# Background projection by halves of a tile, inside a fused attention kernel

## The chip, the cores and the metric

The kernel runs on one core of one Trainium2 chip. The metric is the time of one execution on the device in microseconds (us), as the median of the runs. The engines are TensorE (PE in the profile, with its weight loads as PEld), VectorE (DVE), ScalarE (ACT), GpSimd (POOL) and SyncE (SP), which here only issues transfers.

## The reference, cut to what matters

Two transformer blocks on x of 4 batches x 2048 tokens x 256 features, 16 heads of 16. The change lies in the first attention alone:

```python
q, k, v = split(x @ qkv_w.T)                       # 16 heads of 16
scores = alpha * tanh(q @ k.T / beta)
bits = tanh(x @ hex_w.T); hexc = tanh(x @ q6_w.T)  # 6 + 6 features a token
scores += lam * (bits @ bits.T) / 2 + (hexc @ Mh @ hexc.T) / 6 * gate
out = softmax(causal(scores)) @ v
```

Behind it come the output projection with residual and layer norm, a feed-forward layer, a second attention (rope, plain softmax) and a second feed-forward layer.

## The kernel before, in words

The phases run one after the other: `setup_phase`, `project_phase` (q, k, v and features of batch 0 only), `attend_phase` for layer 0, `middle_phase`, `attend_phase` for layer 1, `post1_phase`. The change is in `attend_phase`, and all but one constant of it concerns layer 0.

**Passes and steps.** A pass (`it`, 16 in all) is one batch and four heads. It has 34 steps (`even_steps`, line 595), each one block of 128 keys against 512 queries for four heads. The queries of a pass are four groups of 512; group 0 ends at step 3, group 1 at 8, group 2 at 20, group 3 at 33. Steps 0, 1, 3, 7, 8, 17, 18, 20, 32 and 33 touch the causal diagonal and add a mask by further matmuls; 1, 3, 8, 18, 20 and 33 of them consist of two pieces. The global step is S = 34 * it + s, up to N = 544.

**A step on each engine, layer 0.** TensorE (from line 892): `weigh(S-2)`, probabilities times v, four heads in 16 matmuls (line 887, bank 6 or 7 by group); `extra(S, 0)` and `extra(S, 1)` (line 864, masks in line 866), the feature part of the scores for two heads; background pieces of place "a"; `scores(S+1)` of four heads (line 854); `extra(S, 2)`; background pieces of place "b"; `extra(S, 3)`. The extra products have two banks in turn: number h waits for VectorE's sum number h-2. ScalarE (line 924): tanh of the scores of S (line 929, 2048 columns), then exp of step S-1 (line 940, 2048 columns), which waits for all four sums of S-1. VectorE, in `sums` (line 993): the copy of a background tile if one ended in this step (`evict`, line 952); sums 0 and 1 (line 1004: alpha * tanh + extra product, read from PSUM); one part of a group's normalisation (`normalise`, line 964); sums 2 and 3. The four parts are a transpose out of PSUM (line 971, counter `o_tr`), a reciprocal (974), a multiplication (978) and a transpose (982, counter `o_n`). The last one waits until the stores of the group before last (`o_out`) have landed, since they read the same buffer `on_s`. Parts become due three steps behind the end of a group, one a step.

**Background projection.** Passes 0 to 11 (NX = 12) also project one group of 512 tokens of a later batch: features (g), q and k in two tiles each, the mixed features f in two tiles, and v in two. The list `plan` gives the places (step and a or b) of the matmuls of each tile. Each tile is copied once, by `evict` at the start of VectorE's step in which its last matmul stands, and the copy waits for that matmul (`bg_ps`). The next tile's first matmul waits for the copy (`bg_ev`). For q, k and f tiles GpSimd then splits the copy in three bf16 parts with four instructions (lines 1033, 1036, 1038, 1040; counters `hi`, `rest`, `mid`, `low`). The feature tile goes through a tanh of ScalarE (line 922) and not through VectorE.

**SyncE's queue** is one list in order (loop in line 781), where each item waits for its counter: at S the load for the group that ended at S-4 (14 transfers, lines 585, 725 and 726, behind `o_tr`); the store of a background tile that ended at S-5; the four stores of the group that ended at S-7 (`store_o`, line 759, transfers of line 765, behind `o_n`).

Of the kernel before, what the change touches and what calls it, by code (L numbers as in the profile page):

```python
# [24 lines left out]
B, T, D = 4, 2048, 256  # L25
# [586 lines left out]
def attend_phase(nc, kn, layer, w=None):  # L612
# [13 lines left out]
    LAG = 2  # L626
    QU, KU = 3, 6
    QK0, E0, O0 = 0, 4, 6
    tiles = [("g", 0), ("q", 0), ("q", 1), ("k", 0), ("k", 1), ("f", 0), ("f", 1)]
    NTL = len(tiles)  # L630
    kinds = tiles + [("v", 0), ("v", 1)]
    NU = len(kinds)
    NX = (B - 1) * GB if layer == 0 else 0
    plan = ["9a 9b", "12a 12b 12b 13a", "13b 14a 14b 15a", "15b 16a 16b 19a", "24a 24b 24b 25a", "25b 26a", "26b 27a", "27b 28a 28b 29a", "29b 30a 30b 31a"]
    slots = {}
    for u, places in enumerate(plan):
        places = places.split()
        for i, p in enumerate(places):
            slots.setdefault(p, []).append((u, i, i == len(places) - 1))
    bank_of = {u: O0 + (1 if 1 <= u <= 3 else 0) for u in range(NU)}  # L640
    behind = {0: 0, 1: 1, 4: 2}
    ahead = {2: 0, 3: 3, 0: 8}

    def pieces(S, place):

        it, s = divmod(S, NST)
        return [(it * NU + u, i, last) for u, i, last in slots.get(f"{s}{place}", [])] if 0 <= it < NX else []

    def unit_at(S):

        ended = [j for j, i, last in pieces(S, "a") + pieces(S, "b") if last]
        return ended[0] if ended else None

    def unit(j):

        X, u = divmod(j, NU)
        kind, m = kinds[u]
        return X, kind, m, X * NTL + u, {"q": P, "k": P, "f": 96, "g": NF, "v": P}[kind], bank_of[u]
    SR, FR = (QROWS, FROWS + 3) if layer == 0 else (QROWS + 3, 0)
    with ExitStack() as ctx:  # L660
        ph = Phase(nc, ctx, f"att{layer}")
# [52 lines left out]
        def _(sp):  # L714
# [18 lines left out]

            def store_unit(j):

                X, kind, m, tile, n, bank = unit(j)
                b, gq = X // GB + 1, X % GB
                if kind == "v":
# [35 lines left out]
            for n in range(QU):  # L774
                load(n)
                if layer == 0 and n == 0:
# [26 lines left out]
        def _(pe):  # L803
# [1 line left out]
                c.start(pe)  # L805
            pe.wait_ge(ones_in, 16)

            def project(j, i, done):

                X, kind, m, tile, n, bank = unit(j)  # L810
                if i == 0:
                    if j == 0:
                        pe.wait_ge(w_in, 64)
# [3 lines left out]
                    if j % NU in behind:  # L817

                        o_tr.wait(pe, X * GB + behind[j % NU])
                half, c = divmod(i, DC)  # L820
                cols = slice(half * D, (half + 1) * D)
                if kind == "f":
                    cols = slice(i * D, (i + 1) * D)
                    mm = pe.matmul(ps[0:n, bank, cols], kn["Cq"][:].rearrange("p q e h -> p (q e h)")[:, m * n:(m + 1) * n], f12[:, X % 2, cols], start=True, stop=True)
                elif kind == "g":
                    mm = pe.matmul(ps[0:n, bank], w12_s[:, c, :], xt_s[:, X % 2, c], start=c == 0, stop=c == DC - 1)
                elif kind == "v":
                    at_t = slice((2 * m + half) * P, (2 * m + half + 1) * P)
                    mm = pe.matmul(ps[:, bank, cols], xt_s[:, X % 2, c, at_t], wv_s[:, c, :], start=c == 0, stop=c == DC - 1)
                else:  # L830
                    lhs = (wq_s if kind == "q" else wk_s)[:, c, m * P:(m + 1) * P]
                    mm = pe.matmul(ps[0:n, bank, cols], lhs, xt_s[:, X % 2, c, cols], start=c == 0, stop=c == DC - 1)  # L832
                if done:
                    bg_ps.done(mm)

            def pieces_at(S, place):
                for j, i, last in pieces(S, place):
                    project(j, i, last)

            def scores(S, pair):  # L840
                it, _, pieces, _ = at(S)
# [50 lines left out]
            for S in range(N + LAG):  # L892
# [4 lines left out]
                if layer == 0 and S < N:  # L897
                    extra(S, 0)
                    extra(S, 1)
                    pieces_at(S, "a")  # L900
                    if S + 1 < N:
                        scores(S + 1, 0)
                if S + 1 < N:
                    scores(S + 1, 1)
                if layer == 0 and S < N:
                    extra(S, 2)
                    pieces_at(S, "b")
                    extra(S, 3)

        @block.scalar  # L910
        def _(act):
# [2 lines left out]

            def feature(j):

                X, kind, m, tile, n, bank = unit(j)
                if kind == "g":
                    bg_ps.wait(act, j)
                    if X >= 2:  # L920
# [22 lines left out]
        def _(dve):  # L943
# [7 lines left out]

            def evict(j):

                X, kind, m, tile, n, bank = unit(j)
# [65 lines left out]
        if layer == 0:  # L1020
            @block.gpsimd
            def _(pool):
                for c in (hi, rest, mid, low):
                    c.start(pool)
                for j in range(NX * NU):
                    X, kind, m, tile, n, bank = unit(j)
                    if kind == "v":
# [1006 lines left out]
```

## Time and profile before

| | us |
|---|---|
| median of 3 runs | 4102.77 (4102.47 to 4106.52) |
| profiled execution | 4100.62 |
| its span, first to last instruction | 4098.8 |
| busy: TensorE / ScalarE / VectorE / GpSimd | 3696.2 / 3502.5 / 2527.2 / 623.6 |
| layer 0 attention, first tanh to last | 133.5 to 2284.9 |
| passes 0 to 11 (with background) | 1653.66 |
| mean granted TensorE clock | 0.97 |

How to read it: busy shares of the whole span mix six phases. For the change only the stretch from 133.5 us to 1787.2 us (passes with background) and on to 2284.9 us (passes 12 to 15, without) counts. A pass is cut from the start of its first tanh to the start of the next pass's. An instruction's duration includes a tail that overlaps the next one, so the distance of two starts is less than a duration. TensorE makes each f32 matmul of the background in two records.

### The profile page before, as it was taken

To read this page: it belongs to the slowest core of one execution; us is meant where nothing else is said; L and a number is where in the kernel's file an instruction comes from. 1 tells how busy PE (TensorE), PEld (TensorE's weight loads), DVE (VectorE), ACT (ScalarE), POOL (GpSimd) and SP (SyncE) were. 2 spreads that over 40 slices of the span, in tenths; PEclk is the share of its full clock that TensorE was granted. 3 is DMA by queue.
4 is the path that set the end of the run, shared out by engine and by line. 5 is a ranking of instruction groups with operands and counts; after the bars stand their busy time and mean duration, and the time that the engine had idled before them with its cause. 6 is when DMAs were issued, how large, how long until landed. Compare 5 with 4: busy or idle time off the path is not lost. (4 is left out here: it accounts for less than half of the span.)

```text
span 4098.8 us, 62490 instructions
## 1 busy us (share of the span) xinstructions
PE 3696.2 (90%) x22198; PEld 1474.5 (36%) x22198; DVE 2527.2 (62%) x4349; ACT 3502.5 (85%) x2970; POOL 623.6 (15%) x659
## 2 busy tenths in 40 slices
PE   5699999999999999999989699969999999999798
PEld 2233333333333333333223366622222222222575
DVE  5577877787778777877788566732232323232576
ACT  2598999998999998999999566659999999999466
POOL 3112121211121112110000055510000000000232
PEclk9799999999999999999999899979999999999899
DMA  4322232222222322221121277642222222221331
GB/s 149 116 72 71 68 87 67 78 66 85 66 75 68 87 69 73 60 85 42 38 60 33 98 191 194 156 110 67 75 72 75 75 74 71 71 78 44 115 93 52
DMA packets 274745, 340.51 MB, mean 83 GB/s; under 512 B 40142, under 2 KB 207918, under 8 KB 274161
## 3 DMA queue, kind: packets, MB, share of 16 engines
q1 hardware_dynamic: 274420, 336.38, 28.1%
q8 instruction: 179, 2.93, 0.3%
q14 instruction: 146, 1.20, 0.1%
HBM read 207.97 MB, written 128.25 MB: 82 GB/s over the span
## 5 line engine op out<-in xcount | busy, mean ns | idle before, releaser
L1004 DVE SCALAR_TENSOR_TENSOR att_prob<-att_tanh,alpha,ps 128x512 f32<-128x512 f32 x2176 | 1513.9, 741 | 348.1 <-ACT att_tanh L929 189.7
L854 PE MATMUL ps<-att_q,att_k 99*128 99x512 bf16 (+5 forms) x5120 | 1138.5, 351 | 84.0 <-DMA att_v<-v_ones 61.2
L887 PE MATMUL ps<-att_prob,att_v 128*32 128x512 f32 (+3 forms) x10240 | 1173.3, 544 | 1.9 <-ACT att_prob L940 1.9
L929 ACT ACTIVATE att_tanh<-ps,rbeta 128x2048 f32<-128x2048 f32 x544 | 1083.4, 1992 | 73.6 <-PE ps L854 63.7
L940 ACT ACTIVATE att_prob<-att_prob 128x2048 f32<-128x2048 f32 x544 | 1053.2, 1936 | 91.7 <-DVE att_prob L1004 90.7
L935 ACT ACTIVATE att_prob<-ps 128x1024 f32<-128x1024 f32 x1088 | 1054.3, 1021 | 25.9 <-PE ps L854 9.8
L864 PE MATMUL ps<-att_f,att_g 75*128 75x512 bf16 (+3 forms) x2560 | 815.2, 357 | 159.4 <-DVE att_prob L1004 148.6
L854 PEld LDWEIGHTS ps<-att_q,att_k 96*128 96x128 bf16 (+1 forms) x5120 | 415.3, 98 | 897.2 <-ACT att_prob L935 427.3
L864 PEld LDWEIGHTS ps<-att_f,att_g 75*128 75x128 bf16 x2560 | 228.8, 97 | 942.9 <-DVE att_prob L1004 908.4
L991 DVE TENSOR_TENSOR att_prob<-att_prob,keep 128x512 f32<-128x512 f32 (+1 forms) x320 | 187.5, 586 | 580.6 <-ACT att_prob L935 579.5
L887 PEld LDWEIGHTS ps<-att_prob,att_v 128*32 128x32 f32 x10240 | 216.8, 108 | 367.1 <-issue 148.4
L1912 POOL TENSOR_SCALAR post_prev<-post_xt,post_om 128x512 f32<-128x512 f32 x64 | 56.8, 905 | 1233.0 <-issue 1124.6
L866 PE MATMUL ps<-mask_kq,identb 128*128 128x128 bf16 x1024 | 212.5, 221 | 0.0
L971 DVE STREAM_TRANSPOSE att_ot<-ps 128x512 f32<-128x512 f32 x128 | 91.2, 712 | 180.3 <-PE ps L887 180.3
L1683 POOL TENSOR_TENSOR mid_x1b<-mid_x,mid_bias 128x256 f32<-128x256 f32 x64 | 44.5, 729 | 626.2 <-ACT mid_x L1282 626.2
L1033 POOL CAST att_parts<-att_raw 128x512 bf16<-128x512 f32 (+1 forms) x72 | 43.8, 609 | 580.3 <-DVE att_raw L962 537.3
L1282 ACT ACTIVATE post_x<-post_rr,post_n_nb,post_n_rs 128x256 f32<-128x256 f32 x128 | 66.4, 589 | 65.6 <-DVE post_n_nb L1271 65.6
L1033 POOL CAST att_parts<-att_f 12x512 bf16<-12x512 f32 x12 | 7.2, 599 | 731.2 <-ACT att_f L922 731.2
L962 DVE COPY att_raw<-ps 128x512 f32<-128x512 f32 (+1 forms) x72 | 49.7, 690 | 98.0 <-PE ps L832 44.5
L1494 ACT ACTIVATE mid_parts<-mid_qcos 128x512 bf16<-128x512 f32 x64 | 40.1, 626 | 81.8 <-POOL mid_qcos L1657 81.6
L866 PEld LDWEIGHTS ps<-mask_kq,identb 128*128 128x128 bf16 x1024 | 101.2, 99 | 2.6 <-issue 0.7
L1040 POOL TENSOR_TENSOR att_parts<-att_rem,att_parts 128x512 bf16<-128x512 f32 (+2 forms) x84 | 97.1, 1156 | 15.1 <-POOL att_parts L1038 15.1
(162 smaller groups left out, 2975.7 us busy)
## 6 DMA issues: line engine op xcount, KB each, us to landing
att_v<-v_ones SPq DMA_DIRECT2D x128, 256.0 KB
att_k<-k_parts SPq DMA_DIRECT2D x128, 192.0 KB
att_q<-q_parts SPq DMA_DIRECT2D x128, 192.0 KB
att_k<-k_parts SPq DMA_DIRECT2D x128, 128.0 KB
att_q<-q_parts SPq DMA_DIRECT2D x128, 128.0 KB
o_t<-att_on SPq DMA_DIRECT2D x512, 32.0 KB, 1.8
v_ones<-mid_vs SPq DMA_DIRECT2D x64, 256.0 KB, 3.3
v_ones<-att_vs SPq DMA_DIRECT2D x96, 128.0 KB, 2.1
```

The source lines that it names most:

```text
L854: mm = pe.matmul(ps[:, bank, col:col + w], keys, q_s[:, n % QU, h, q0:q0 + w], start=True, stop=True)
L864: mm = pe.matmul(ps[:, E0 + h % 2, col:col + w], g_s[:, c % KU, (kb % CB) * P:(kb % CB + 1) * P], f_s[:, n % QU, h, q0:q0 + w], start=True ...
L866: mm = pe.matmul(ps[:, E0 + h % 2, col:col + P], kn["identb"][:], kn["mask_kq"][:], start=False, stop=True)
L887: mm = pe.matmul(ps[VW * h:VW * (h + 1), O0 + n % 2, q0:q0 + w], v_s[:, c % KU, kb % CB, h * VW:(h + 1) * VW], prob[:, S % R, h, col:col + ...
L929: th.done(act.activation(tanh_s[:, S % 2], ps[:, QK0:QK0 + HQ], ACT.Tanh, scale=kn["rbeta"][:, 0:1]))
L935: pr.done(act.activation(prob[:, S % R, 2 * pair:2 * pair + 2], ps[:, bank:bank + 2], ACT.Exp, scale=float(HD) ** -0.5))
L940: pr.done(act.activation(prob[:, (S - 1) % R], prob[:, (S - 1) % R], ACT.Exp))
L971: o_tr.done(dve.transpose(ot_s[:, v].rearrange("p b n -> p (b n)"), ps[:, O0 + v]))
L991: kept.done(dve.tensor_tensor(block, block, kn["keep"][:].unsqueeze(1).unsqueeze(1).to_broadcast([P, 2, len(masked), P]), ALU.min))
L1004: sc.done(dve.scalar_tensor_tensor(prob[:, S % R, h], tanh_s[:, S % 2, h], kn["alpha"][:, 0:1], ps[:, E0 + h % 2], ALU.mult, ALU.add))
L1040: low.done(pool.tensor_tensor(parts[0:n, u, 2], rem[0:n], parts[0:n, u, 1], ALU.subtract))
L1282: ins = act.activation(dst(t), src(t), ACT.Identity, scale=self.rs[:, u, t:t + 1], bias=self.nb[:, u, t:t + 1])
```

## The change

Each q, k and v tile is now projected by halves: a unit of `plan` is a half tile of 256 columns with exactly two matmuls, one in a place "b" and one in the next step's "a", so there are 15 units a pass instead of 9, with 30 matmuls as before. The two f tiles and the feature tile stay whole. The order of the tiles is g, q0, k0, f0, f1, q1, k1, v0, v1. Each unit is copied by itself: at steps 13, 14, 15, 16 (halves), 19, 20 (f), 25 to 31 and 32 (halves). Before, whole tiles were copied at 13, 15, 19, 25, 26, 27, 29 and 31. Splitting in parts and storing still go by whole tiles, after the second half. A step that has a copy does no part of a normalisation; the feature tile doesn't count. In layer 0 the stores of a group stand 14 steps behind its end in SyncE's list instead of 7.

```diff
-    plan = ["9a 9b", "12a 12b 12b 13a", "13b 14a 14b 15a", "15b 16a 16b 19a", "24a 24b 24b 25a", "25b 26a", "26b 27a", "27b 28a 28b 29a", "29b 30a 30b 31a"]
+    plan = [("g", 0, None, "9a 9b"), ("q", 0, 0, "12b 13a"), ("q", 0, 1, "13b 14a"), ("k", 0, 0, "14b 15a"), ("k", 0, 1, "15b 16a"),
+            ("f", 0, None, "16b 19a"), ("f", 1, None, "19b 20a"), ("q", 1, 0, "24b 25a"), ("q", 1, 1, "25b 26a"), ("k", 1, 0, "26b 27a"),
+            ("k", 1, 1, "27b 28a"), ("v", 0, 0, "28b 29a"), ("v", 0, 1, "29b 30a"), ("v", 1, 0, "30b 31a"), ("v", 1, 1, "31b 32a")]
...
-    behind = {0: 0, 1: 1, 4: 2}
-    ahead = {2: 0, 3: 3, 0: 8}
+    behind = {0: 0, 1: 1, 7: 2}
+    ahead = {2: 0, 3: 6, 0: 14}
...
-            for S in range(N + 8):
+            BACK = 14 if layer == 0 else 7
+            for S in range(N + BACK):
...
-                if 7 <= S < N + 7:
-                    it, s, *_ = at(S - 7)
+                if S >= BACK:
+                    it, s, *_ = at(S - BACK)
                     for g in ends[s]:
                         store_o(it * GB + g)
...
-                    bg_ev.done(dve.tensor_copy(vs[:, m, :, :, 0:HD], ps[:, bank].rearrange("p (t h d) -> p t h d", t=2, h=H)))
+                    bg_ev.done(dve.tensor_copy(vs[:, m, half, :, 0:HD], ps[:, bank, cols].rearrange("p (h d) -> p h d", h=H)))
...
-                    bg_ev.done(dve.tensor_copy(raw[0:n, tile % 2], ps[0:n, bank]))
+                    bg_ev.done(dve.tensor_copy(raw[0:n, tile % 2, cols], ps[0:n, bank, cols]))
...
+                copied = unit_at(S)
+                if copied is not None and unit(copied)[1] == "g":
+                    copied = None
                 for h in range(HQ):
-                    if h == 0 and unit_at(S) is not None:
-                        evict(unit_at(S))
-                    if h == 2:
+                    if h == 0 and copied is not None:
+                        evict(copied)
+                    if h == 2 and copied is None:
 
                         normalise(due, 1)
```

## Rows read from the trace of the kernel before

**Rows 1.** Busy time of stretches (start:end, length; busy by engine; PEclk, DMA share, GB/s)

```profile
133.53:275.98 142.45, 125.37 (x736) 47.68 (x734) 104.53 (x154) 125.67 (x69) 24.70 (x28) 0.94 0.30 88
414.77:549.63 134.86, 123.50 (x765) 47.21 (x764) 107.50 (x161) 126.92 (x71) 24.71 (x28) 1.00 0.25 75
549.63:688.43 138.80, 127.96 (x765) 47.92 (x764) 107.71 (x161) 126.91 (x71) 24.68 (x28) 0.96 0.25 73
sum 1653.66, PE 1515.02 PEld 572.44 DVE 1287.49 ACT 1521.80 POOL 296.47; mean PE 126.25 PEld 47.70 DVE 107.29 ACT 126.82 POOL 24.71
1911.39:2035.71 124.32, 112.48 (x705) 36.26 (x705) 99.91 (x152) 124.32 (x69) 0.00 (x0) 1.00 0.17 51
383.10:393.34 10.24, 10.24 (x31) 2.75 (x31) 4.92 (x9) 5.93 (x4) 5.94 (x7) 0.50 0.29 82
```

**Rows 2.** Waits of ScalarE in pass 2: total us, times, longest

```profile
ACT att_prob L940 <- DVE att_prob L1004: 7.2, 8, 1.9
```

**Rows 3.** Timeline of pass 2, steps 30 and 31: start, us, engine, line, tiles [idle before]

```profile
535.97 0.60 PE L864 MATMUL ps<-att_f,att_g 75*128 75x512 bf16 x2
...
539.67 0.60 PE L864 MATMUL ps<-att_f,att_g 75*128 75x512 bf16 x2
540.12 0.60 PE L829 MATMUL ps<-att_wv,att_xt 128*128 128x256 f32 x2
540.80 0.69 DVE L958 COPY att_vs<-ps 128x512 f32<-128x512 f32 x1 [1.20 <-PE ps L829]
541.41 2.71 DVE L1004 SCALAR_TENSOR_TENSOR att_prob<-att_tanh,alpha,ps 128x512 f32<-128x512 f32 x4
...
542.87 0.39 PE L864 MATMUL ps<-att_f,att_g 75*128 75x512 bf16 x1 [0.27 <-DVE att_prob L1004]
543.19 1.06 PE L887 MATMUL ps<-att_prob,att_v 128*32 128x512 f32 x8
544.16 1.91 ACT L940 ACTIVATE att_prob<-att_prob 128x2048 f32<-128x2048 f32 x1 [0.58 <-DVE att_prob L1004]
544.18 0.39 PE L864 MATMUL ps<-att_f,att_g 75*128 75x512 bf16 x1
```

**Rows 4.** Timeline of pass 2, the masked steps 32 and 33

```profile
544.75 1.04 PE L854 MATMUL ps<-att_q,att_k 96*128 96x128 bf16 x8
544.77 2.81 DVE L1004 SCALAR_TENSOR_TENSOR att_prob<-att_tanh,alpha,ps 128x512 f32<-128x512 f32 x4 [0.64 <-PE ps L866]
...
548.26 2.92 DVE L1004 SCALAR_TENSOR_TENSOR att_prob<-att_tanh,alpha,ps 128x512 f32<-128x512 f32 x4 [0.68 <-PE ps L866]
```

**Rows 5.** Timelines of pass 2, steps 25 and 26, and of pass 13 (last row)

```profile
515.45 1.15 POOL L1036 TENSOR_TENSOR att_rem<-att_raw,att_parts 128x512 f32<-128x512 f32 x1 [0.28 <-POOL att_parts L1033]
515.53 1.35 DVE L978 TENSOR_TENSOR att_oq<-att_ot,att_rc 128x256 f32<-128x256 f32 x1
...
518.58 0.67 PE L824 MATMUL ps<-att_f,Cq 12*96 12x256 f32 x2
...
519.34 0.69 DVE L962 COPY att_raw<-ps 96x512 f32<-96x512 f32 x1 [1.14 <-issue]
...
1962.43 0.42 DVE L978 TENSOR_TENSOR att_oq<-att_ot,att_rc 128x256 f32<-128x256 f32 x1
```

**Rows 6.** Timeline of pass 13, step 14; last row: landing of the stores of o

```profile
1965.17 0.36 SPq L726 DMA_DIRECT2D att_v<-v_ones  x1
...
1966.09 0.70 DVE L982 STREAM_TRANSPOSE att_on<-att_oq 128x512 f32<-128x512 f32 x1
...
1966.88 1.71 SPq L765 DMA_DIRECT2D o_t<-att_on  x4
...
DMA to landing us min/median/max: 1.5/1.7/2.8
```

**Rows 7.** Timeline of ScalarE in pass 2, tanh of steps 9 and 11

```profile
447.63 2.01 ACT L929 ACTIVATE att_tanh<-ps,rbeta 128x2048 f32<-128x2048 f32 x1
...
455.71 1.95 ACT L929 ACTIVATE att_tanh<-ps,rbeta 128x2048 f32<-128x2048 f32 x1
```

More of the change, by code:

```diff
@@ L628, in attend_phase, with piece_at @@
     QK0, E0, O0 = 0, 4, 6
-    tiles = [("g", 0), ("q", 0), ("q", 1), ("k", 0), ("k", 1), ("f", 0), ("f", 1)]
+    tiles = [("g", 0), ("q", 0), ("k", 0), ("f", 0), ("f", 1), ("q", 1), ("k", 1)]
     NTL = len(tiles)
-    kinds = tiles + [("v", 0), ("v", 1)]
-    NU = len(kinds)
     NX = (B - 1) * GB if layer == 0 else 0
-    plan = ["9a 9b", "12a 12b 12b 13a", "13b 14a 14b 15a", "15b 16a 16b 19a", "24a 24b 24b 25a", "25b 26a", "26b 27a", "27b 28a 28b 29a", "29b 30a 30b 31a"]
[L635 to L640, printed above, removed]
-    behind = {0: 0, 1: 1, 4: 2}
-    ahead = {2: 0, 3: 3, 0: 8}
-    def pieces(S, place):
+    plan = [("g", 0, None, "9a 9b"), ("q", 0, 0, "12b 13a"), ("q", 0, 1, "13b 14a"), ("k", 0, 0, "14b 15a"), ("k", 0, 1, "15b 16a"),
+            ("f", 0, None, "16b 19a"), ("f", 1, None, "19b 20a"), ("q", 1, 0, "24b 25a"), ("q", 1, 1, "25b 26a"), ("k", 1, 0, "26b 27a"),
+            ("k", 1, 1, "27b 28a"), ("v", 0, 0, "28b 29a"), ("v", 0, 1, "29b 30a"), ("v", 1, 0, "30b 31a"), ("v", 1, 1, "31b 32a")]
+    NU = len(plan)
+    places = {p: (u, i) for u, (_, _, _, both) in enumerate(plan) for i, p in enumerate(both.split())}
+    behind = {0: 0, 1: 1, 7: 2}
+    ahead = {2: 0, 3: 6, 0: 14}
+    def piece_at(S, place):
         it, s = divmod(S, NST)
-        return [(it * NU + u, i, last) for u, i, last in slots.get(f"{s}{place}", [])] if 0 <= it < NX else []
+        if not 0 <= it < NX or f"{s}{place}" not in places:
+            return None
+        u, i = places[f"{s}{place}"]
+        return it * NU + u, i
     def unit_at(S):
-        ended = [j for j, i, last in pieces(S, "a") + pieces(S, "b") if last]
+        ended = [found[0] for found in (piece_at(S, "a"), piece_at(S, "b")) if found and found[1] == 1]
         return ended[0] if ended else None
@@ L656, in unit @@
         X, u = divmod(j, NU)
-        kind, m = kinds[u]
-        return X, kind, m, X * NTL + u, {"q": P, "k": P, "f": 96, "g": NF, "v": P}[kind], bank_of[u]
+        kind, m, half, _ = plan[u]
+        tile = X * NTL + tiles.index((kind, m)) if kind != "v" else None
+        return X, kind, m, half, tile, {"q": P, "k": P, "f": 96, "g": NF, "v": P}[kind], O0 + (1 if 1 <= u <= 6 else 0)
     SR, FR = (QROWS, FROWS + 3) if layer == 0 else (QROWS + 3, 0)
@@ L734, in store_unit @@
             def store_unit(j):
-                X, kind, m, tile, n, bank = unit(j)
+                X, kind, m, half, tile, n, bank = unit(j)
                 b, gq = X // GB + 1, X % GB
+                if half == 0:
+                    return
                 if kind == "v":
@@ L806, in _, with project @@
             pe.wait_ge(ones_in, 16)
-            def project(j, i, done):
-                X, kind, m, tile, n, bank = unit(j)
+            def project(j, i):
+                X, kind, m, half, tile, n, bank = unit(j)
                 if i == 0:
@@ L825, in project, with piece @@
                 elif kind == "g":
[L826 to L829, printed above, removed]
-                else:
-                    lhs = (wq_s if kind == "q" else wk_s)[:, c, m * P:(m + 1) * P]
-                    mm = pe.matmul(ps[0:n, bank, cols], lhs, xt_s[:, X % 2, c, cols], start=c == 0, stop=c == DC - 1)
-                if done:
+                    mm = pe.matmul(ps[0:n, bank], w12_s[:, i, :], xt_s[:, X % 2, i], start=i == 0, stop=i == DC - 1)
+                else:
+                    cols = slice(half * D, (half + 1) * D)
+                    if kind == "v":
+                        lhs, rhs = xt_s[:, X % 2, i, (2 * m + half) * P:(2 * m + half + 1) * P], wv_s[:, i, :]
+                    else:
+                        lhs, rhs = (wq_s if kind == "q" else wk_s)[:, i, m * P:(m + 1) * P], xt_s[:, X % 2, i, cols]
+                    mm = pe.matmul(ps[0:n, bank, cols], lhs, rhs, start=i == 0, stop=i == DC - 1)
+                if i == 1:
                     bg_ps.done(mm)
-            def pieces_at(S, place):
-                for j, i, last in pieces(S, place):
-                    project(j, i, last)
+            def piece(S, place):
+                if piece_at(S, place):
+                    project(*piece_at(S, place))
             def scores(S, pair):
@@ L915, in feature @@
             def feature(j):
-                X, kind, m, tile, n, bank = unit(j)
+                X, kind, m, half, tile, n, bank = unit(j)
                 if kind == "g":
@@ L952, in evict @@
             def evict(j):
-                X, kind, m, tile, n, bank = unit(j)
+                X, kind, m, half, tile, n, bank = unit(j)
+                cols = slice(None) if half is None else slice(half * D, (half + 1) * D)
                 if kind == "v":
@@ L1025, in _ @@
                 for j in range(NX * NU):
-                    X, kind, m, tile, n, bank = unit(j)
-                    if kind == "v":
+                    X, kind, m, half, tile, n, bank = unit(j)
+                    if kind == "v" or half == 0:
                         continue
```

6 lines of the change are left out of this document (2 added, 4 removed).

## Prediction

> **What bounds the kernel now.** I read the page first: no single engine bounds the whole, so the stage is read by itself. Next come the stretches cut at the first tanh of each pass of 34 steps [rows 1]. A pass without background work takes 124.32 us, that is 3.66 us a step, and ScalarE is busy for all of it: one tanh and one exp of 2048 columns a step. So ScalarE sets the rate there. A pass with background work takes 134.86 us, but ScalarE is busy for 126.92 only. The waits of ScalarE in that pass name what it waits for: 8 waits for VectorE's sums, 7.2 us [rows 2]. There are 8 copies in a pass, so it is the copies that the change splits.
>
> Three things make up the 1653.66 us of the twelve passes. Five passes have a granted clock of 1.00 and take 134.9 to 135.2 us; the seven others have 0.94 to 0.96 and take some 138.8 [rows 1]. In those seven the clock falls to 0.50 (1.2 GHz instead of 2.4) for 10.24 us, once a pass, behind the steps in which TensorE waited most. The fall costs 138.80 - 134.86 = 3.94 us. Pass 0 has another 142.45 - 134.86 = 7.6 us of starting up. What is left, 1653.66 - 7.6 - 12 x 134.86 = 27.7 us, is the price of the lower clock. And a clean pass has 134.86 - 124.32 = 10.5 us of background.
>
> **Why a copy costs what it does.** The timeline of step 31 of pass 2 [rows 3] shows a loop through two engines. The second sum ends, the last extra product of the step starts (542.87), the weighing of an older step starts 0.32 later (543.19) and lasts 0.99 (544.18), two extra products take 0.45 (539.67 to 540.12), then comes the background piece; the copy starts 0.68 behind the start of its piece (540.80), the first sum 0.61 later (541.41). Two sums take 1.41, and the signal to TensorE 0.05. Once around with a full copy: 1.41 + 0.05 + 0.32 + 0.99 + 0.45 + 0.68 + 0.61 = 4.51 us. ScalarE's exp waits 0.58 us (544.16) for the fourth sum. Nothing in the loop is hidden by slack elsewhere: VectorE's sum of work is well under 3.65 us a step, and its queue still waits 1.20 us for the piece.
>
> **The change, part by part.** *Half copies.* 8 full copies a pass become 12 copies of 256 columns and 2 full ones (f). VectorE works on another operation of 256 columns for 0.42 us [rows 5], against 0.69 for 512 [rows 3]; I take the difference, 0.27, off the link: 0.34. A loop with a half copy then takes 4.24 us, 0.59 more than ScalarE's 3.65. Between bounds of 0.34 and 0.61 for the link I take 0.34, since both rows fit 1.05 ns a column. *First copy of a run (steps 13 and 25).* Before it stands a step with ScalarE's slack; working through it with one piece instead of two in the step before, the fourth sum is ready 0.07 us before exp wants it: 0. *The next ones* (14, 15, 16 and 26 to 31): 9 x 0.59 - 2 x 0.07 = 5.2 us. *Step 32* is masked: extra products and masks take 0.57 (544.18 to 544.75) instead of 0.45, the four sums 2.81 instead of 2.71 [rows 3, 4]: 4.46 - 3.65 = 0.8. *The f copies* stay full and stand at steps 19 and 20. A piece of f takes 0.67 against 0.60, and its copy starts 0.76 behind it [rows 5]. At 19 the transpose of the normalisation, 0.70 [rows 6], was just before in step 18 and delays the fourth sum, the second extra product and so the piece: worked through in the same way, the loop is 0.7 over. Step 20 has two pieces of mask (first sums 3.49 apart instead of 3.36 [rows 3, 4], so extra products of 0.70) and follows a copy step: 4.51 + 0.70 - 0.45 + 0.08 + 0.09 for slower sums + 0.1 for the extra product that f's piece makes late = 5.03, so 1.4 over. *Normalisation moved* to steps 17, 18, 33 and 0 of the next pass, all masked. First sum to first sum takes 3.36 and 3.49 us there; adding 0.42 and then 0.70 - 0.42, they come to 0.3 + 0.2 + 0.25 + 0.1 = 0.9. Sum of a new pass: 5.2 + 0.8 + 2.1 + 0.9 = 9.0, and the feature tile, which stays as it was: two steps from 447.63 to 455.71 instead of 7.30 [rows 7], 0.8. So 9.8 against 10.5: 0.77 us a pass before rounding, 9.2 us in twelve.
>
> What goes away and makes room for this: the multiplication in a copy step takes 1.35 us beside GpSimd's subtraction, 0.42 alone [rows 5]. After the change no such pair meets: at step 17 GpSimd's last subtraction of the k tile ends some 0.3 us before it. What this pair cost stands in the old 10.5 and not in the new 9.8.
>
> The Trainium skill speaks against this change ("VectorE: DVE Perf Modes", on the TRN2 errata): each instruction pays a fixed latency, many small tiles pay it each time, and a copy from PSUM costs 120 cycles plus one per column. The estimate from that page is 0.39 us for a half and 0.66 for a full copy; the full one's 0.69 in the trace agrees. By it, with the whole half copy in the link, a pass would be 12 x 0.05 = 0.6 us dearer, twelve of them 7 us.
>
> *Clock.* The longest stop in the passes, 1.85 us of ScalarE behind the 1.35 us multiplication, is gone; the new loops leave TensorE waiting some 0.5 us a step, as steps 29 to 33 do now at full clock. I take all 27.7 us as saved.
>
> *Stores of o, 14 steps behind instead of 7.* SyncE's queue is in order, so its place matters. The store of group 3 now stands behind the load of group 1 of the next pass, whose 14 transfers SyncE issues until 1965.17 + 0.36 = 1965.53 in pass 13 [rows 6]. Passes with copies normalise group 1 at steps 17 and 18, later than that. Passes 12 to 15 have no copies, and there the last transpose is due at step 14, at 1966.09, and it waits for those very stores, which share its buffer. Now they were made before the load. Four stores take 1.71 us to issue and land 1.7 us (up to 2.8) behind their issue: 1965.6 + 1.3 + 1.7 = 1968.6, 2.5 us late; up to 3.6 with the load's own traffic in front. Queued behind the transpose are sums 3 and 4, and ScalarE's exp and TensorE behind them. I take 2.8 us, near the usual landing, in passes 12, 13 and 14 (15 has no such load): +8.4 us. TensorE stands idle for over 2 us in each, longer than where the clock falls now; I take two falls of 3.5 us (3.94, less the background's share): +7.
>
> *The rest*: tile order, banks and the waits on o_tr stay behind events that came steps earlier; GpSimd has the same 28 instructions a pass. Price 0; a missed one would cost up to 0.6 us a pass, one late cast.
>
> **Sum.** On the profiled execution, 4100.62 us (span 4098.8): -9.2 - 27.7 + 8.4 + 7 = -21.5, 4079. The median of the runs shown is 2.15 above it: 4081.3, **4081 us**.
>
> **The rivals.** *Copies in the slack* (0.04): counted as work, a half copy fits, and the step would be as long as TensorE's, 3.70 with two pieces (535.97 to 539.67 [rows 3]). A pass then has 14 x 0.05 + 0.8 = 1.5 us of background, 8.3 less than forecast: 4081 - 12 x 8.3, near 3980. Against it stands the loop, whose every link is in order. *No late store* (0.13): had GpSimd's or SyncE's order left the buffer free, no +8.4 and +7: 4066. *Dearer links* (0.14): 0.1 us on each of 14 links in 12 passes is 17 us: 4098. *The clock falls all the same* (0.14), which ends slower: the new run of eight steps at 4.24 us has a gap of TensorE in each, and if these bring the clock down in as many passes as now, 4081 + 27.7 = 4109, in all twelve 4128. Other terms add up to +6, so the change is slower once the clock falls in six passes or more. Against it: the single steps of 4.36 to 4.5 us now run at full clock. The Trainium skill ("TensorE: Matmul & The Clock Gate", on a second failure mode) says that short, frequent idling between groups of matmuls can make the clock oscillate; the trace agrees so far that gaps of at most 0.6 us of TensorE precede the falls here. *It does nothing that counts*: part of the last two.
>
> **How the numbers follow.** My forecast has 0.55, the rivals as given. The range takes in no late store below and dearer links above, with room for landing times and one fall more or less: 4064 to 4102. A measurement of this kernel tells about 0.2%, 8.2 us, from no change, so faster means under 4094.6: forecast, cheap copies, no late store (0.72), plus 0.06 of the others, 0.78. Slower needs falls in most passes: 0.10. The rest, 0.12, is the same.
>
> **What would show it.** In passes 0 to 11: first sums 4.2 to 4.3 us apart at steps 26 to 31, 5.0 to 5.1 from 19 to 20, pass time about 134.1, clock 1.00, no multiplication over 0.5 us. In passes 12 to 14: one gap of VectorE before line 982's transpose at step 14, of 2.5 to 3.6 us, released by the stores of o, none in pass 15. It would be wrong if the loop were shorter than 4.1, if the clock rows showed 0.96 in many of the twelve passes, or if that transpose didn't wait.

## The result and the profile after

The changed kernel takes 4095.8 us (median of 20 runs, 4092.45 to 4106.26) against 4102.62 us before (20 runs, 4099.94 to 4106.62): ratio 0.9984, with a 95% interval of 0.9977 to 0.9991. So it is faster by 7 us, as that interval shows, where 21.5 were forecast; the prediction called faster only what is under 4094.6 us, and by this bound it is no change. The profiled execution took 4096.26 us.

The page and the cut by passes, for the changed kernel. The first group is of the page (busy us, share, instructions), the rows under it are busy times of stretches as in [rows 1]: passes 0 to 11 together, passes 12 to 14, then pass 2, pass 6 and a stretch inside pass 2.

```profile
span 4094.4 us, 62634 instructions
PE 3699.9 (90%) x22198; PEld 1468.8 (36%) x22198; DVE 2497.9 (61%) x4421; ACT 3515.6 (86%) x2970; POOL 623.8 (15%) x659
...
134.65:1771.96 1637.31, 1512.80 (x9139) 564.99 (x9138) 1256.50 (x1984) 1533.69 (x828) 296.58 (x336) 0.98 0.25 74
...
1771.96:2155.47 383.51, 342.35 (x2116) 110.13 (x2114) 301.24 (x459) 374.05 (x206) 0.00 (x0) 0.98 0.18 53
...
413.35:550.72 137.37, 128.03 (x766) 47.78 (x764) 104.96 (x167) 127.97 (x71) 24.73 (x28) 0.96 0.24 74
...
954.51:1088.46 133.95, 123.73 (x766) 46.33 (x764) 104.96 (x167) 127.76 (x70) 24.71 (x28) 1.00 0.25 76
...
490.85:501.09 10.24, 10.24 (x50) 3.68 (x49) 4.70 (x7) 5.57 (x4) 5.89 (x7) 0.50 0.01 3
```

A pass without a fall of the clock is now 133.95 to 134.2 us long, where the sum said 134.1 and the kernel before had 134.86 [rows 1]. But the clock still falls, in 8 of the 12 passes instead of 7, though often for a shorter time: 1637.31 - 7.6 (start of pass 0) - 12 x 134.0 = 21.7 us against 27.7 before. Passes 12 to 14 took

```profile
1787.19:2160.06 372.87, 337.22 (x2114) 108.77 (x2114) 299.77 (x457) 372.87 (x206) 0.00 (x0) 1.00 0.18 51
```

in the kernel before (the row is of its trace), so they are now 10.6 us longer. In sum: twelve passes -16.4 us, three passes +10.6 us, and 1.4 us elsewhere (the first tanh starts 1.1 us later): -4.4, the difference of the two profiled executions.

### The profile page after: what moved, and what is told of

It is laid out like the page before. It is cut to its first block and busy times, and to the rows that moved or that the text cites. A ratio compares the mean times of both kernels' runs of the same rounds, so it can differ in the third digit from the quotient of the medians.

```text
span 4094.4 us, 62634 instructions
## 1 busy us (share of the span) xinstructions
PE 3699.9 (90%) x22198; PEld 1468.8 (36%) x22198; DVE 2497.9 (61%) x4421; ACT 3515.6 (86%) x2970; POOL 623.8 (15%) x659
## 3 DMA queue, kind: packets, MB, share of 16 engines
q1 hardware_dynamic: 274420, 336.38, 27.7%
## 5 line engine op out<-in xcount | busy, mean ns | idle before, releaser
L965 DVE COPY att_raw<-ps 128x256 f32<-128x256 f32 (+1 forms) x120 | 57.2, 477 | 156.5 <-PE ps L834 86.0
```

## The loop, as it now runs

Timeline of pass 6, steps 26 and 27, of the changed kernel (start, us, engine, line, operation, tiles; idle time before in brackets):

```profile
1058.22 2.71 DVE L1010 SCALAR_TENSOR_TENSOR att_prob<-att_tanh,alpha,ps 128x512 f32<-128x512 f32 x4
...
1060.00 1.06 PE L889 MATMUL ps<-att_prob,att_v 128*32 128x512 f32 x8
...
1060.97 1.91 ACT L942 ACTIVATE att_prob<-att_prob 128x2048 f32<-128x2048 f32 x1 [0.31 <-DVE att_prob L1010]
...
1061.44 0.60 PE L834 MATMUL ps<-att_xt,att_wk 128*128 128x256 f32 x2
...
1062.12 0.42 DVE L965 COPY att_raw<-ps 128x256 f32<-128x256 f32 x1 [1.19 <-PE ps L834]
1062.47 2.71 DVE L1010 SCALAR_TENSOR_TENSOR att_prob<-att_tanh,alpha,ps 128x512 f32<-128x512 f32 x4
```

First sum to first sum: 1062.47 - 1058.22 = 4.25 us, forecast 4.24. The half copy takes 0.42 us, and the next sum starts 0.35 us behind its start, which is what it takes in the loop. VectorE is idle for 1.19 us before a copy that takes 0.42, and ScalarE for 0.31 us in each step of this run. What ScalarE waits for in pass 6:

```profile
ACT att_prob L942 <- DVE att_prob L1010: 5.1, 13, 0.7
```

Thirteen waits of 5.1 us together, where 8 of 7.2 stood [rows 2]: shorter ones, but more of them. The multiplication of the normalisation, 1.35 us beside GpSimd before [rows 5], keeps its 0.42 us throughout (min/median/max in ns):

```profile
L981 DVE TENSOR_TENSOR att_oq<-att_ot,att_rc x128: 415/424/427, 175.2 to 3794.1; 128x256 f32<-128x256 f32 x128
```

## The stall in passes 12 to 14

Timeline of pass 13, step 14, changed kernel:

```profile
1952.95 0.35 SPq L726 DMA_DIRECT2D att_v<-v_ones  x1
...
1953.43 5.58 SPq L767 DMA_DIRECT2D o_t<-att_on  x12
...
1956.51 0.71 DVE L985 STREAM_TRANSPOSE att_on<-att_oq 128x512 f32<-128x512 f32 x1 [2.57 <-DMA o_t<-att_on]
...
1957.91 0.39 PE L866 MATMUL ps<-att_f,att_g 75*128 75x512 bf16 x1 [2.52 <-DVE att_prob L1010]
1958.55 1.91 ACT L942 ACTIVATE att_prob<-att_prob 128x2048 f32<-128x2048 f32 x1 [2.44 <-DVE att_prob L1010]
```

The waits of VectorE in passes 12 to 14 (total us, times, longest):

```profile
DVE att_on L985 <- DMA o_t<-att_on: 7.7, 3, 2.6
```

The stores begin right behind the load, the transpose waits 2.57 us for them, and TensorE and ScalarE wait behind it. It happens three times and never in pass 15, as the prediction had it.

**Experiment: stores 11 steps behind.** The smallest number that puts the stores of group 3 before the load of group 1 and still keeps SyncE from waiting long for the delayed normalisations.

```diff
-            BACK = 14 if layer == 0 else 7
+            BACK = 11 if layer == 0 else 7
```

> The changed kernel with the stores of o 11 steps behind the end of a group in the first attention instead of 14, so that the stores of group 3 stand before the load of group 1 again. Theory (the stall is the place in SyncE's list): passes 12 to 14 fall from 127.3, 128.8 and 127.4 us to 124.3 each, the wait of VectorE before the last transpose at step 14 is gone, and so are the falls of the clock there; passes 0 to 11 stay. 10.7 us faster than the changed kernel, 17 faster than the kernel before (ratio 0.996). Rival (the store lands late whatever its place, or the half-clock stretches there come from elsewhere): passes 12 to 14 stay over 126 us.

Measured: 4086.25 us, ratio 0.996 to the kernel before (0.9946 to 0.9974), 9.6 us under the changed kernel's median. Passes 12 to 14, and all twelve passes before them:

```profile
1774.11:2147.17 373.06, 337.58 (x2116) 108.93 (x2113) 300.72 (x459) 373.05 (x205) 0.00 (x0) 1.00 0.19 55
...
134.14:1774.11 1639.97, 1517.32 (x9139) 565.83 (x9138) 1256.05 (x1984) 1534.02 (x827) 296.56 (x336) 0.97 0.25 74
```

The three passes are back at 373.06 us with a clock of 1.00. The wait of VectorE before the last transpose is gone. The stall cost 10.4 us, and its cause is shown: the place of four stores in one queue. The twelve passes before are 2.7 us longer than in the changed kernel, as ten of them lose the clock here and eight there, with the same instructions in them.

## What brings the clock down

The prediction let the clock stay up once the 1.85 us stop was gone. It falls in the changed kernel as well, but elsewhere: at steps 20 and 21 instead of 27. Timeline of pass 2 from the end of step 18 into step 20, TensorE's matmuls alone:

```profile
487.98 0.67 PE L825 MATMUL ps<-att_f,Cq 12*96 12x256 f32 x2
...
490.14 0.39 PE L866 MATMUL ps<-att_f,att_g 75*128 75x512 bf16 x1 [0.51 <-DVE att_prob L1010]
490.46 0.82 PE L825 MATMUL ps<-att_f,Cq 12*96 12x256 f32 x2
...
491.75 1.94 PE L889 MATMUL ps<-att_prob,att_v 128*32 128x128 f32 x16
...
495.01 1.16 PE L825 MATMUL ps<-att_f,Cq 12*96 12x256 f32 x2
```

The largest gap of TensorE here is 0.51 us; then the weighing takes 1.94 us instead of 1.06. In both kernels the two f tiles stand where the clock falls, and their matmuls feed 12 of TensorE's 128 rows (12*96 in the row). Two theories: A, it is these few rows, in steps that wait; B, it is the length of the waits. In the kernel before, steps 14 and 26 have the same stop of ScalarE, 1.85 us each. Their rows in pass 2:

```profile
467.01:472.65 5.64, 4.22 (x22) 1.86 (x23) 5.64 (x8) 3.78 (x2) 3.54 (x4) 1.00 0.35 109
514.42:520.25 5.83, 4.65 (x20) 1.33 (x20) 4.69 (x7) 3.88 (x2) 3.53 (x4) 1.00 0.54 166
```

TensorE is idle for 1.42 us in step 14 and for 1.18 in step 26. Step 14 has q pieces of 128 rows and no fall follows it in twelve passes; step 26 has f and a fall follows it in seven. That speaks for A. Five runs tell them apart.

**Experiment: f exchanged with the halves of q1.**

```diff
-    tiles = [("g", 0), ("q", 0), ("k", 0), ("f", 0), ("f", 1), ("q", 1), ("k", 1)]
+    tiles = [("g", 0), ("q", 0), ("k", 0), ("q", 1), ("f", 0), ("f", 1), ("k", 1)]
...
-            ("f", 0, None, "16b 19a"), ("f", 1, None, "19b 20a"), ("q", 1, 0, "24b 25a"), ("q", 1, 1, "25b 26a"), ("k", 1, 0, "26b 27a"),
+            ("q", 1, 0, "16b 19a"), ("q", 1, 1, "19b 20a"), ("f", 0, None, "24b 25a"), ("f", 1, None, "25b 26a"), ("k", 1, 0, "26b 27a"),
```

> The changed kernel with the two f tiles and the halves of q1 exchanged: q1's halves are copied at steps 19 and 20, f0 and f1 at steps 25 and 26. Theory A (the clock falls behind the pieces of f, which feed 12 of TensorE's 128 rows, when two tiles of f follow each other in long steps): the falls move from steps 20 and 21 to steps 26 and 27, in about as many passes, and step 20 is some 4.7 us without a fall. Theory B (it is the long masked step 20 with its waits): falls stay at steps 20 and 21. Sum without clock: step 20 shorter by 0.35, step 26 longer by 0.35: pass times without a fall within 0.3 us of 134.0 either way. Time within 10 us of the changed kernel.

Measured: 4092.82 us, ratio 0.9979 (0.9969 to 0.9989), 3 us from the changed kernel. Steps 19 to 23 and 24 to 29 of pass 6:

```profile
1024.60:1044.13 19.53, 17.60 (x122) 6.85 (x120) 14.94 (x24) 18.61 (x11) 3.54 (x4) 1.00 0.03 8
...
1044.13:1073.40 29.27, 27.77 (x115) 8.82 (x114) 18.43 (x30) 22.85 (x14) 10.59 (x12) 0.83 0.28 84
```

The falls went with f: none at 20 and 21, five at step 26 (passes 1, 3, 6, 9 and 11). Whether the place has a part in the lower number isn't shown: two kernels with the same steps 19 to 21 have eight and ten.

**Experiment: f's matmuls over 128 rows, in the changed kernel.**

```diff
-                    mm = pe.matmul(ps[0:n, bank, cols], kn["Cq"][:].rearrange("p q e h -> p (q e h)")[:, m * n:(m + 1) * n], f12[:, X % 2, cols], start=True, stop=True)
+                    mm = pe.matmul(ps[0:n, bank, cols], wq_s[:, 0, 0:n], xt_s[:, X % 2, 0, cols], start=True, stop=True)
```

> The changed kernel with f's matmuls replaced: the same number, 96 columns of weights and 256 columns of data, but over 128 rows (wq and x) instead of 12 (Cq and the features), so the mixed features of batches 1 to 3 are left out and wrong data are copied and stored in their place; all copies, waits and stores stay. Theory A (few rows of TensorE at work bring the clock down): no fall in passes 0 to 11, twelve pass times of 134 us or a little less, 21 us faster than the changed kernel, near 4075. Theory B (TensorE's waits alone do it): falls stay at steps 20 and 21 in about 8 passes and the time stays within 5 us.

Measured: 4063.04 us, ratio 0.9906 (0.9889 to 0.9922). Pass 2, and the twelve passes:

```profile
406.22:539.36 133.14, 122.72 (x766) 46.48 (x764) 104.83 (x167) 127.72 (x70) 24.73 (x28) 1.00 0.26 76
...
134.02:1739.01 1604.99, 1474.30 (x9139) 559.15 (x9138) 1253.53 (x1984) 1531.29 (x828) 296.79 (x336) 1.00 0.26 76
```

No fall in twelve passes. It came 12 us under what I expected, 10 of them because the pieces are also shorter (a pass is 133.14 instead of 134.0). So this run alone leaves B a door: the steps were shorter. In passes 12 to 14, which have no f, the falls behind the 2.5 us stall stayed: a long enough wait does it without any f.

**Experiment: the same in the kernel before.** The same line of the diff.

> The kernel before with the same replacement of f's matmuls by ones over 128 rows (mixed features of batches 1 to 3 left out, wrong data copied and stored in their place). Theory A (long steps bring the clock down only where the few-row pieces of f stand in them): no fall of the clock, twelve passes of 134 to 135 us, some 27.7 us and the shorter pieces of f off, near 4070. Theory B (the 1.85 us stop of ScalarE was what brought it down in the kernel before): falls stay at step 27 in about 7 passes, within 10 us of the kernel before.

Measured: 4069.39 us, ratio 0.9913 (0.9896 to 0.993). Steps 24 to 29 of pass 2:

```profile
501.12:527.42 26.30, 23.14 (x119) 9.05 (x118) 20.23 (x31) 22.65 (x14) 10.58 (x12) 1.00 0.34 101
```

The same stretch of pass 3 in the kernel before, where the clock falls:

```profile
641.63:672.20 30.57, 28.62 (x119) 9.61 (x118) 20.49 (x31) 22.87 (x13) 10.57 (x12) 0.83 0.34 97
```

No fall either, and the 1.85 us stop is still there (step 26 takes 5.64 us against 5.84). B said about 7 falls.

**Experiment: f over 128 rows and longer.** With the stores 11 steps behind, each f matmul stands twice.

```diff
-                    mm = pe.matmul(ps[0:n, bank, cols], kn["Cq"][:].rearrange("p q e h -> p (q e h)")[:, m * n:(m + 1) * n], f12[:, X % 2, cols], start=True, stop=True)
+                    for _ in range(2):
+                        mm = pe.matmul(ps[0:n, bank, cols], wq_s[:, 0, 0:n], xt_s[:, X % 2, 0, cols], start=True, stop=True)
```

> The changed kernel with the stores 11 steps behind and each matmul of f replaced by two over 128 rows (mixed features of batches 1 to 3 left out, wrong data stored in their place), so that a piece of f holds TensorE longer than in the changed kernel, some 0.87 us, and steps 19 and 20 are as long as with the true f or longer (5.2 us or more at 20). Theory A (few rows at work): no fall of the clock in passes 0 to 11 although the steps are no shorter. Theory B (falls went away before only because the pieces and steps were shorter): falls at steps 20 and 21 in several passes.

Measured: 4074.05 us, ratio 0.9928 (0.9906 to 0.9951). Steps 19 and 20 of pass 5, and the twelve passes:

```profile
887.39:897.14 9.75, 8.97 (x64) 4.62 (x64) 6.11 (x10) 7.71 (x5) 3.52 (x4) 1.00 0.19 55
...
132.86:1759.90 1627.04, 1495.91 (x9235) 574.98 (x9234) 1256.15 (x1984) 1533.02 (x828) 296.40 (x336) 0.99 0.25 75
```

Steps 19 and 20 are longer than in the changed kernel (9.75 us against 9.12 with the true f, in the row of the next experiment; step 20 alone 5.63 against 5.17, with a gap of TensorE of 0.62 us against 0.51), and there is no fall in any pass. (The mean of 0.99 is of the end of a low stretch at the very start of pass 0, which all kernels have.) That closes B's door in so far as longer steps and longer gaps are not enough, though these pieces also keep TensorE busy longer.

**Experiment: the pieces of q1 and k1 over 12 rows.** The other direction, with the true f and the stores 11 steps behind; the same number of matmuls, with the same columns, but 12 rows.

```diff
+                    if kind != "v" and m == 1:
+                        lhs, rhs = lhs[0:NF], rhs[0:NF]
                     mm = pe.matmul(ps[0:n, bank, cols], lhs, rhs, start=i == 0, stop=i == DC - 1)
```

> The changed kernel with the stores 11 steps behind and, in addition to f, the pieces of q1 and k1 (steps 24 to 28) cut to 12 of their 128 rows (queries and keys of half the heads' rows of batches 1 to 3 are projected from 12 features only and wrong). Theory A (few-row pieces in steps that wait): falls of the clock appear at steps 25 to 29 too, in some passes, beside those at 20 and 21; passes of 136 us and more. Theory B (few rows don't matter, the length of the waits does): the steps 25 to 28 keep 4.24 us, falls stay at steps 20 and 21 alone.

Measured (two runs): 4177.24 us, ratio 1.0183 (1.0125 to 1.0242). Steps 19 and 20 and steps 24 to 29 of pass 5, and the pass itself:

```profile
928.92:938.04 9.12, 8.46 (x58) 3.46 (x58) 6.21 (x10) 7.71 (x6) 3.52 (x4) 1.00 0.19 58
...
951.03:986.45 35.42, 34.92 (x115) 9.67 (x114) 18.26 (x30) 22.89 (x13) 7.07 (x8) 0.66 0.23 69
...
856.55:1003.49 146.94, 138.16 (x766) 47.93 (x764) 105.76 (x167) 128.18 (x70) 24.70 (x28) 0.91 0.24 69
```

Steps 24 to 29 of pass 6 in the changed kernel:

```profile
1047.66:1071.42 23.76, 22.06 (x115) 8.38 (x114) 17.55 (x30) 22.67 (x13) 7.08 (x8) 1.00 0.32 103
```

Six steps that took 23.76 us at full clock take 35.42: the clock is at its lower level for two thirds of them. It falls there in 9 of 12 passes, for 23.9 us in seven and 17.1 in two. Not all of the difference is the clock. Pass 8 keeps it, and its steps 24 to 29 take

```profile
1390.76:1416.45 25.69, 24.41 (x115) 7.61 (x114) 17.91 (x30) 22.90 (x13) 7.07 (x8) 1.00 0.30 95
```

that is 1.9 us more than with 128 rows, since a piece of 12 rows lasts longer: 0.63 us from its start to the next matmul (958.95 to 959.58) against 0.43 (1061.44 to 1061.87). The weight load of the piece of 128 rows starts 0.22 us before its first matmul, that of 12 rows together with it (first row of the changed kernel, the others of pass 5 here, before the fall):

```profile
1061.22 0.41 PEld L834 LDWEIGHTS ps<-att_xt,att_wk 128*128 128x128 f32 x2
...
958.95 0.29 PEld L836 LDWEIGHTS ps<-att_xt,att_wq 12*128 12x128 f32 x2 [0.23 <-issue]
958.95 0.69 PE L836 MATMUL ps<-att_xt,att_wq 12*128 12x256 f32 x2
```

So with 12 rows TensorE is by its rows busier (24.41 of 25.69 us against 22.06 of 23.76) and its gap in a step is shorter (0.26 us against 0.36), and the clock falls all the same, where it never does with 128 rows. A stands against B: the gaps alone don't do it. It is not told apart whether the rows at work count or the weight load that no longer runs ahead of its matmul. And few rows alone don't do it either: where TensorE hardly waits, and they stand one in a step, they bring no fall (the experiment with the copy out of the loop, below).

## Which part of the change pays, and which costs

**Experiment: the normalisation moved, tiles whole.** The kernel before, with these lines and the stores 11 steps behind.

```diff
+                copied = unit_at(S)
+                if copied is not None and unit(copied)[1] == "g":
+                    copied = None
                 for h in range(HQ):
-                    if h == 0 and unit_at(S) is not None:
-                        evict(unit_at(S))
-                    if h == 2:
+                    if h == 0 and copied is not None:
+                        evict(copied)
+                    if h == 2 and copied is None:
```

> The kernel before with one part of the change alone: a step with a copy does no normalisation (whole tiles and the old order stay), and the stores of o stand 11 steps behind. Theory (halving costs, moving the normalisation gains): the 1.35 us multiplication is gone and six whole q, k and v copies cost 0.86 each against twelve halves of 0.59, so a clean pass takes about 132 us against 134.05 of the changed kernel and 134.86 before: some 4060 with a few falls of the clock. Rival (halving is what gains): clean passes stay at or above 134.05 us, and the time above the changed kernel's 4096.

Measured: 4051.42 us, ratio 0.9884 (0.9867 to 0.99), 44 us under the changed kernel. Pass 11 and the twelve passes:

```profile
1607.31:1740.52 133.21, 123.04 (x765) 47.00 (x764) 105.83 (x161) 127.16 (x71) 24.66 (x28) 1.00 0.25 72
...
134.10:1740.52 1606.42, 1481.70 (x9140) 565.90 (x9138) 1266.08 (x1914) 1524.98 (x828) 295.98 (x336) 0.99 0.26 77
```

A clean pass is 132.9 to 133.3 us, some 1.1 above what I expected and 1 below the changed kernel; and the clock falls in one pass of twelve. Of the 31 us by which the twelve passes are shorter than the changed kernel's, some 12 are the length of a clean pass and most of the others the clock. The 1.35 us multiplication is gone, though ten passes have one of 0.5 to 1.08 us at step 28. This run also shows that the stop counted: with f at the same steps as in the kernel before and over the same 12 rows, but step 26 at 5.04 us instead of 5.84, the falls went from seven passes to one. So the falls of the kernel before took both, the few-row pieces and the stop. Why one pass still loses the clock was not looked into.

**Experiment: halves, but a normalisation in every step.** The changed kernel with the stores 11 steps behind.

```diff
-                    if h == 2 and copied is None:
+                    if h == 2:
```

> The changed kernel with the stores 11 steps behind and one part of the change undone: a step with a copy also does its part of a normalisation. Theory (with halves GpSimd starts later, so the multiplication at steps 13 and 25 does not meet it, and moving the normalisation buys little): no multiplication over 0.5 us, a clean pass 134.0 to 135 us, time within 12 us of the 4086 of the changed kernel with the stores 11 steps behind. Rival (moving it is what saves, with halves as with whole tiles): a 1.35 us multiplication is back and clean passes are over 136 us, 4110 or more.

Measured: 4079.03 us, ratio 0.9939 (0.9923 to 0.9956): 7 us under the same kernel with the normalisation moved (4086.25). Pass 2 of this kernel:

```profile
412.58:547.07 134.49, 124.04 (x766) 46.29 (x764) 105.30 (x167) 127.37 (x71) 24.70 (x28) 1.00 0.25 76
```

A clean pass is 0.5 us longer, but only one pass in twelve has a fall of the clock, where the same kernel with the normalisation moved has them in ten. Step 20 is as long in both (5.17 us, with the same gap of TensorE of 0.51 us); near f only steps 18 and 19 differ (3.65 and 3.76 us here, 3.71 and 3.95 there). What in this decides on the fall stays open. No multiplication is over 0.43 us here. So, by the clean passes of these kernels, a pass is 134.9 us (neither), 133.0 (moved), 134.5 (halves), 134.0 (both): the two parts do not add, and the halves take back 1 us of the 1.9 that moving the normalisation gives.

**Experiment: the copy out of the loop.** Whole tiles, with the lines of the experiment before last, but the copy between the second and the third sum, and each tile beginning one place after the copy of the last.

```diff
-    plan = ["9a 9b", "12a 12b 12b 13a", "13b 14a 14b 15a", "15b 16a 16b 19a", "24a 24b 24b 25a", "25b 26a", "26b 27a", "27b 28a 28b 29a", "29b 30a 30b 31a"]
+    plan = ["9a 9b", "12a 12b 12b 13a", "14a 14b 14b 15a", "16a 16b 16b 19a", "24a 24b 24b 25a", "26a 27a", "28a 29a", "30a 30b 30b 31a", "32a 32b 32b 33a"]
...
-                    if h == 0 and copied is not None:
+                    if h == 2 and copied is not None:
                         evict(copied)
```

> Whole tiles in the old order, normalisation not in copy steps, stores 11 steps behind, and the copy moved from before the first sum to between the second and the third, where a normalisation part would stand; the next tile begins one place later (a instead of b), so that TensorE doesn't wait for the copy. Theory (the loop from second sum over weighing, extra products and piece to copy and first sum is what a copy costs): a copy out of the loop costs nothing, steps with three pieces cost 0.35 us, a clean pass is about 127.5 us instead of 134, and the time near 3985. Rival (the four engines are simply full, so that the copy's 0.69 us count wherever they stand): a clean pass stays over 132 us and the time over 4045.

Measured: 3997.66 us, ratio 0.9741 (0.9725 to 0.9757), 98 us under the changed kernel. Pass 2 and the twelve passes:

```profile
397.62:526.12 128.50, 122.87 (x767) 47.41 (x765) 106.47 (x161) 126.91 (x70) 24.71 (x28) 1.00 0.26 79
...
134.73:1683.35 1548.62, 1475.59 (x9139) 569.12 (x9138) 1274.21 (x1914) 1522.12 (x828) 296.43 (x336) 1.00 0.27 79
```

The timeline of VectorE in a step of pass 5, and the waits of ScalarE in a stretch a little longer than a pass (942.11 to 1075.0):

```profile
894.14 1.41 DVE L1008 SCALAR_TENSOR_TENSOR att_prob<-att_tanh,alpha,ps 128x512 f32<-128x512 f32 x2 [0.36 <-ACT att_tanh L930]
895.46 0.68 DVE L963 COPY att_raw<-ps 96x512 f32<-96x512 f32 x1
896.11 1.41 DVE L1008 SCALAR_TENSOR_TENSOR att_prob<-att_tanh,alpha,ps 128x512 f32<-128x512 f32 x2
```

```profile
ACT att_prob L941 <- DVE att_prob L1008: 0.4, 1, 0.4
```

The copy is as long as before (0.68 us), with no wait in front of it, and ScalarE waits 0.4 us for the sums instead of 7.2 (4.4 in the same stretch of the kernel with whole tiles and the copy in its old place). The same 8 whole copies, 28 instructions of GpSimd and 30 background matmuls cost 4.2 us a pass instead of 10.5. No pass loses the clock, although f's pieces have 12 rows here as well. They stand one in each of steps 26 to 29, and TensorE is idle for 0.21 us in step 26 and for 0.04 in each of the others. It is the fastest kernel of this study; I had it 1 us a pass shorter, mostly the masked step 33, which now holds a piece and a copy.

**Experiment: the half copies late, with the old list of pieces.** The changed kernel with the stores 11 steps behind and `h == 2` for the copy.

> The changed kernel with the stores 11 steps behind and the copies between the second and the third sum; the list of pieces stays, so the next piece, in place b, waits for the copy. Theory (loop): 1.41 + copy 0.34 + signal 0.05 + piece 0.44 + 0.32 + 0.99 + 0.53 = 4.08 us from first sum to first sum in steps 26 to 31 instead of 4.24, passes without a fall about 132, some 20 us faster than the 4086 of the same kernel with early copies. Rival (engines full): 4.24 us and 4086 as before.

Measured: 4054.86 us, ratio 0.9886 (0.987 to 0.9903), 31 us under the same kernel with early copies. Pass 7:

```profile
1076.29:1208.28 131.99, 124.34 (x766) 46.62 (x765) 106.92 (x167) 127.58 (x71) 24.70 (x28) 1.00 0.25 77
```

The timeline of steps 28 and 29 of that pass:

```profile
1187.67 0.42 DVE L965 COPY att_raw<-ps 128x256 f32<-128x256 f32 x1
...
1188.14 0.70 PE L834 MATMUL ps<-att_wv,att_xt 128*128 128x256 f32 x2 [0.20 <-DVE att_raw L965]
...
1191.83 0.42 DVE L961 COPY att_vs<-ps 128x256 f32<-128x256 f32 x1
```

The step is 1191.83 - 1187.67 = 4.16 us, between my 4.08 and the old 4.24, since the piece behind the wait takes 0.54 us of TensorE (1188.14 to the next extra product at 1188.68) and not 0.44. The pass is the 132 us I expected, which makes some 24 of the 31 us; the time is 11 us under the 4066 I had expected, and seven passes lose the clock here instead of ten, behind gaps of TensorE of at most 0.35 us in six of the seven. The loop is confirmed from a second side: it now closes through the wait of the next piece, 0.20 us.

## Why the prediction was right or wrong

- *ScalarE sets the pace, the copies break it*: right. With the normalisation moved and the whole copies out of the loop the twelve passes went from 1653.66 [rows 1] to 1548.62 us, that is 105 of the 162 us by which they had exceeded 12 x 124.32, and ScalarE was left with almost no wait. By the clean passes (134.9, 133.0, 128.6 us), some 53 of the 105 are the place of the copy and 23 the normalisation; most of the others are the clock's 27.7.
- *The loop, 4.51 us with a full and 4.24 with a half copy*: right to 0.01 us. Single steps: 5.03 expected from 19 to 20, 5.17 measured in clean passes; steps 17, 18, 33 and 0 came to 0.7 + 0.1 + 0.5 + 0.1 = 1.4 against 0.9, and 32 to 0.8.
- *A new pass of 134.1 us*: 134.0 measured.
- *The multiplication beside GpSimd*: right, none is over 0.43 us. The Trainium skill ("SBUF — State Buffer", on the port pair that VectorE and GpSimd share) says the one that comes second is blocked for the whole instruction of the other; the trace of before agrees, as the multiplication began 0.08 us behind the subtraction and ended 0.28 behind its end [rows 5].
- *The late stores*: right in mechanism, place and number. The wait is 2.57 us, forecast 2.5 to 3.6 with 2.8 taken. The term was +15.4 with two falls of the clock at 3.5 us; it measured +10.6, because the clock did fall in all three passes but for 3.4 to 6.8 us, which cost some 3 us together and not 7.
- *The clock*: wrong, and this is the step that failed: "I take all 27.7 us as saved." It saved 6. The reason given was that the 1.85 us stop goes and that the new loops wait no more than steps 29 to 33 do at full clock. But those steps hold no matmul of few rows, and the change lets both f tiles end in steps 19 and 20, of which step 20 is the longest of the new pass (5.17 us). There the clock falls in eight passes. What the runs showed in place of the assumption is that the falls go with f's few-row matmuls, in steps with gaps: none with f over 128 rows, in either kernel, and f moved to steps 25 and 26 took the falls to step 26. The stop did count in the kernel before (seven passes with it, one without it); the new kernel has falls without it. The row that could have warned stood in the trace of before: step 14 has the same stop and no fall. The prediction has the falls "behind the steps in which TensorE waited most"; TensorE waited more in step 14 (1.42 us) than in step 26 (1.18). It also counts five passes at a clock of 1.00 where there are four; pass 0 has 0.94 without a fall of its own, which leaves the 27.7 as they are.
- *The rival that the clock falls all the same* (0.14) named the right effect in the wrong place: the run of eight steps at 4.24 us keeps its clock. Its price of +27.7 was too high, since many falls became shorter, and its bound, slower from six passes on, didn't hold: eight passes lose the clock and the kernel isn't slower.
- *The sum*: -9.2 became -10.3 (12 x 0.86), -27.7 became -6, +15.4 became +10.6, and 1.4 came in elsewhere: -4.3 against -21.5, where the two profiled executions are 4.4 apart and the medians 7. The range held, and the direction by the interval of the ratio, though not by the prediction's own bound of 4094.6; the size did not. That the time still lies in the range is in part luck: the range had room for one fall more or less, and eight came, many of them shorter than those before, beside a stall 5 us cheaper than forecast.
- *That half copies pay*: the sum gave the whole change 0.8 us a pass without saying that one of its parts loses. Both prices were there: 0.86 for a full copy and 2 x 0.59 for its halves.

## What to carry to other kernels

Price a small operation by what it waits for and who waits for it: a copy of 0.69 us cost 0.86 us a time in the one place and, by the waits it left (0.4 us a pass), almost nothing 1.4 us later in the same step, and cutting it in two made two turns of the same loop. Before a loss of the clock is counted as saved, look for a place with the same wait and no fall; what differs there is the first suspect, and where the change puts it has to be looked at too. And when a store is moved back in a queue in order, write down what it now stands behind in the stretches where nothing else was changed.

## What was not expected of the hardware

TensorE's clock follows more than whether the engine has matmuls. With the same number of matmuls and the same columns, steps 24 to 29 run at 1.00 with 128 rows at work (22.06 us busy of 23.76). With 12 rows in eight of the pieces the profile shows the engine busier (24.41 of 25.69 us in a pass that keeps the clock), and yet in nine of twelve passes the clock of these steps falls, to a mean of 0.66 in pass 5 (34.92 of 35.42). The Trainium skill ("TensorE: Matmul & The Clock Gate", on what actually happens) puts the gate's state down to how busy the engine has been, and the trace agrees in so far as a stall of 2.5 us brings it to 0.50 in passes without any few-row piece. That matmuls of 12 rows count otherwise than the same ones of 128 is shown by the runs with f over 128 rows and by this one. Whether it is the rows or their later weight load stays open, and so does how they weigh against gaps and why a pass with the same pieces keeps its clock one time and loses it the next.
